# A three-pass feature-interaction kernel: second weights loaded one slot later, first weights in other buffers, one contraction row moved, chunk loops written out

## The reference

```python
# r_x: (2048, 39, 16); W0: (1, 39*39, 128); W1: (1, 39*128, 128)
x0 = x
xk = x
outs = []
for W in (W0, W1):
    Hk = xk.shape[1]                       # 39, then 128
    Wr = W.reshape(m, Hk, Hn)              # Hn = 128
    xk = jnp.einsum('bid,bjd,ijh->bhd', x0, xk, Wr)
    outs.append(xk)
result = jnp.concatenate(outs, axis=1)
return jnp.sum(result, axis=-1)            # (2048, 256)
```

## Time and profile before

| | us |
|---|---|
| median of 3 runs | 658.65 (657.7 to 661.69) |
| the profiled execution, its own time | 659.25 |
| its span (the trace) | 657.1 |
| busy in the span: PE / POOL / ACT / DVE | 577.2 / 482.4 / 475.5 / 469.9 |
| moved by DMA | 163.91 MB, mean 249 GB/s |

### The profile page before, as it was taken

One profiled execution on the slowest core, in us unless ns is written; L12 is line 12 of the kernel. 1 busy time (PEld: TensorE's weight loads), 2 busy tenths in 40 slices (PEclk: granted clock), 3 DMA queues, 4 the chain that ended last, 5 costly groups with the idle time before them and its releaser, 6 DMA issues.

```text
span 657.1 us, 12616 instructions
## 1 busy us (share of the span) xinstructions
PE 577.2 (88%) x3176; PEld 500.0 (76%) x3176; DVE 469.9 (72%) x806; ACT 475.5 (72%) x983; POOL 482.4 (73%) x407
## 2 busy tenths in 40 slices
PE   2475566677899999999997999999999999999988
PEld 1254445566788888888886888888888888888878
DVE  4564555455588888888886788888888888888730
ACT  4364645555688888888886888888888888888730
POOL 6765656555788888888885888888888889888700
PEclk9597787778899999999998999999999999999989
DMA  8865566666988899989996898989989898988110
GB/s 285 308 178 175 158 194 181 197 193 209 286 293 278 287 303 296 285 287 298 302 289 214 281 292 291 271 275 321 300 281 297 300 304 286 305 294 284 47 37 17
DMA packets 66357, 163.91 MB, mean 249 GB/s; under 512 B 10096, under 2 KB 18544, under 8 KB 66288
## 3 DMA queue, kind: packets, MB, share of 16 engines
q1 hardware_dynamic: 66288, 163.09, 77.7%
HBM read 139.98 MB, written 2.10 MB: 216 GB/s over the span
## 4 chain that ended last, share of the span: by engine, by line
PE 71%; DMA 13%; ACT 7%; DVE 3%; SPq 3%; issue 3%; POOL 1%; ACTq 0%; DVEq 0%
PE acc L361 13%; DMA xdr<-xd_dram 11%; PE acc L363 11%; PE acc L362 11%; PE fin L401 5%; PE fin L402 5%; PE fin L403 5%; PE pg L387 5%; PE pg L388 5%; PE pg L389 5%; PE turn L373 3%; ACT fh L454 3%; PE acc L356 2%; SPq L245 1%; DMA xr<-xb_dram 1%
## 5 line engine op out<-in xcount | busy, mean ns | idle before, releaser
L691 POOL TENSOR_TENSOR fl<-fs,fh 128x512 fp32r<-128x512 f32 x192 | 248.6, 1297 | 54.0 <-ACT fh L454 51.2
L361 PE MATMUL acc<-fh,w0h 128*128 128x512 f32 x384 | 170.5, 444 | 67.2 <-ACT x L475 49.6
L591 DVE TENSOR_TENSOR fl<-fp,fh 128x512 fp32r<-128x512 f32 x192 | 131.9, 687 | 84.7 <-ACT fh L454 80.9
L686 POOL TENSOR_TENSOR fs<-xr,xs 128x512 f32<-128x512 f32 x128 | 163.0, 1295 | 6.2 <-DMA xr<-xb_dram 6.2
L363 PE MATMUL acc<-fl,w0h 128*128 128x512 f32 x384 | 158.0, 411 | 0.0
L587 DVE TENSOR_TENSOR fp<-xl,xr 128x512 f32<-128x512 f32 x192 | 133.4, 696 | 34.3 <-ACT xl L461 24.0
L362 PE MATMUL acc<-fh,w0l 128*128 128x512 f32 x384 | 157.6, 410 | 0.0
L605 DVE TENSOR_TENSOR gl<-pg,gh 128x320 fp32r<-128x320 f32 x256 | 119.2, 486 | 38.7 <-ACT gh L494 36.2
L454 ACT ACTIVATE fh<-fp 128x512 fp32r<-128x512 f32 x192 | 114.1, 594 | 43.2 <-PE acc L363 38.4
L361 PEld LDWEIGHTS acc<-fh,w0h 128*128 128x128 f32 x384 | 76.0, 198 | 90.6 <-ACT x L475 53.2
L454 ACT ACTIVATE fh<-fs 128x512 fp32r<-128x512 f32 x192 | 121.0, 630 | 9.0 <-PE acc L363 7.6
(11 more groups left out here) (38 smaller groups left out, 748.5 us busy)
## 6 DMA issues: line engine op xcount, KB each, us to landing
xr<-xb_dram SPq DMA_DIRECT2D x192, 512.0 KB, 5.7
xbd<-xdhl SPq DMA_DIRECT2D x256, 80.0 KB, 3.8
xs<-xa_dram SPq DMA_DIRECT2D x64, 256.0 KB, 3.5
xdr<-xd_dram SPq DMA_DIRECT2D x64, 160.0 KB, 5.7
xp<-xpairs_dram SPq DMA_DIRECT2D x32, 256.0 KB, 3.9
outs<-w_dram SPq DMA_DIRECT2D x9, 256.0 KB, 2.7
out_dram<-outs SPq DMA_DIRECT2D x8, 256.0 KB, 5.0
xr<-w0a_dram SPq DMA_DIRECT2D x2, 256.0 KB, 5.2
```

The source lines that it names most:

```text
L361: nc.tensor.matmul(acc[:, :], w0h[:, t, :], fh[:, t, :], start=t == 0, stop=False)
L591: nc.vector.tensor_tensor(fl[:, t, :], f_at(t), fh[:, t, :], ALU.subtract).then_inc(low_dve, 1)
L686: nc.gpsimd.tensor_tensor(f_at(t), xr[:, gi % 2, t, :], xs[:, gi % 2, :], ALU.mult)\
L691: nc.gpsimd.tensor_tensor(fl[:, t, :], f_at(t), fh[:, t, :], ALU.subtract).then_inc(low_pool, 1)
```

## The change

1. `w1_load(g+1)` at the end of SP's slot g (from slot 0 on) becomes `w1_load(g)` (from slot 1 on). `w1_load(0)`, ahead of the slots, now stands behind a wait for `w0_ready` 3.
2. The first weights' raw pieces lie in other buffers: w0a in the tile of POOL's product 4 and in `outs`, w0b in `outs` and `x1`. SP's and POOL's order at the start is changed with it; the first squares and `low(0, 5)` are done ahead of slot 0.
3. Of each slot's rows of the contraction the first (EARLY = 1) is done behind quarters 0 and 1, ahead of `main` of tile 0; in the slots gi = 1 all five stay where they were.
4. The loops over chunks are written out on all engines.

```diff
--- before.py
+++ after.py
@@ -46,13 +46,15 @@
 W0_PART = 4
 W0_FROM = {0: 1, W0_PART: 2, FULL: 3}
 NW = 4
+EARLY = 1
 PIECES = -(-M // NW)
 
 
-def rows_of(s):
-
-
-    return range(IB * (s - 1), min(IB * s, M))
+def rows_of(s, late):
+
+
+    cut = IB * (s - 1) + (EARLY if s > 1 else 0)
+    return range(cut, min(IB * s, M)) if late else range(IB * (s - 1), cut)
 
 
 def piece(p):
@@ -141,9 +143,9 @@
         turn = ps("turn", [P, GC])
         xl = ps("xl", [P, GC])
         fp = ps("fp", [P, 2, GC])
-        w0a_raw = [xr[:, 1, NT - 2 + k, :].rearrange("p (t h) -> p t h", h=H) for k in range(2)]
-        w0b_raw = [outs[:, :, :].rearrange("p a b -> p (a b)").rearrange("p (t h) -> p t h", h=H),
-                   x1[:, :].rearrange("p (t h) -> p t h", h=H)]
+        outs_as_w = outs[:, :, :].rearrange("p a b -> p (a b)").rearrange("p (t h) -> p t h", h=H)
+        w0a_raw = [fs[:, SBUF_F[4], :].rearrange("p (t h) -> p t h", h=H), outs_as_w]
+        w0b_raw = [outs_as_w, x1[:, :].rearrange("p (t h) -> p t h", h=H)]
 
         ident_in = sem("ident_in")
         w0_sum = sem("w0_sum")
@@ -251,10 +253,11 @@
             def load_xd(g):
                 sp.dma_start(xdr[:, :, :, :], xd[g]).then_inc(xd_in, 16)
 
-            def w0_load(k):
-                ts = slice(W0_PART * k, W0_PART * k + W0_PART)
-                sp.dma_start(w0a_raw[k], w0a[:, ts, :]).then_inc(w0a_in[k], 16)
-                sp.dma_start(w0b_raw[k], w0b[:, ts, :]).then_inc(w0b_in[k], 16)
+            def w0a_load(k):
+                sp.dma_start(w0a_raw[k], w0a[:, W0_PART * k:W0_PART * k + W0_PART, :]).then_inc(w0a_in[k], 16)
+
+            def w0b_load(k):
+                sp.dma_start(w0b_raw[k], w0b[:, W0_PART * k:W0_PART * k + W0_PART, :]).then_inc(w0b_in[k], 16)
 
             def w1_load(p):
                 if p:
@@ -302,25 +305,27 @@
                         sp.wait_ge(xd_low, g + 2)
                     if more2:
                         load_xd(g + 2)
-                    if first or second and g + 1 < PIECES:
-                        w1_load(g + 1)
+                    if (first or second) and 0 < g < PIECES:
+                        w1_load(g)
                     if gi == 2 and not (first or second):
                         send(j - 2)
 
-            w0_load(0)
+            w0a_load(0)
+            w0b_load(0)
             load_x(0, 0)
             load_right(0, 0, 0)
             load_right(0, 0, 1)
-            w0_load(1)
+            w0b_load(1)
             load_right(0, 0, 2)
             load_pair(0)
-            load_xd(0)
             load_x(0, 1)
             load_right(0, 1, 0)
+            sp.wait_ge(w0_ready, 1)
+            w0a_load(1)
+            load_right(0, 1, 1)
+            load_right(0, 1, 2)
+            load_xd(0)
             sp.dma_start(idn[:, :], ident).then_inc(ident_in, 16)
-            load_right(0, 1, 1)
-            sp.wait_ge(w0_ready, 3)
-            load_right(0, 1, 2)
             wait_product(sp, 0, 0)
             wait_product(sp, 0, 4)
             load_x(0, 2)
@@ -331,11 +336,11 @@
             load_right(0, 2, 2)
             sp.wait_ge(xd_low, 1)
             load_xd(1)
-            sp.wait_ge(w0_sum, 1)
+            sp.wait_ge(w0_ready, 3)
             w1_load(0)
             chunk(0, True, False, False)
             chunk(1, False, True, False)
-            with sp.Fori(2, NCH - 1) as j:
+            for j in range(2, NCH - 1):
                 chunk(j, False, False, False)
             chunk(NCH - 1, False, False, True)
             send(NCH - 2)
@@ -389,6 +394,8 @@
                 nc.tensor.matmul(o, x1tl[:, q, :], xh, start=False, stop=True).then_inc(g_done, 1)
 
             def final(c, odd, rows, fresh):
+                if not rows:
+                    return
                 if rows[0] == 0:
                     pe.wait_ge(g_low, CB * NQ * (c + 1))
                     if not fresh:
@@ -404,6 +411,12 @@
                     if i == M - 1:
                         last.then_inc(fin_done, 1)
 
+            def last_rows(j, gi, first, second, odd, late):
+                if gi and not first:
+                    final(j - 1, not odd, rows_of(gi, late), second)
+                if not gi and not (first or second):
+                    final(j - 2, odd, rows_of(CB, late), False)
+
             def chunk(j, first, second, last, odd):
                 for gi in range(CB):
                     g = CB * j + gi
@@ -411,6 +424,7 @@
                     if not (first and gi < 2):
                         for q in (0, 1):
                             g_tile(j, gi - 2, q, first and gi == 2)
+                    last_rows(j, gi, first, second, odd, False)
                     main(j, gi, 0, fresh)
                     main(j, gi, 1, fresh)
                     if not (first and gi < 2):
@@ -422,22 +436,17 @@
                     main(j, gi, 3, fresh)
                     main(j, gi, 4, fresh)
                     main(j, gi, 5, fresh)
-                    if gi and not first:
-                        final(j - 1, not odd, rows_of(gi), second)
-                    if not gi and not (first or second):
-                        final(j - 2, odd, rows_of(CB), False)
+                    last_rows(j, gi, first, second, odd, True)
                     main(j, gi, FULL, fresh)
 
             chunk(0, True, False, False, False)
             chunk(1, False, True, False, True)
-            with pe.Fori(1, NCH // 2 - 1) as pair:
-                chunk(2 * pair, False, False, False, False)
-                chunk(2 * pair + 1, False, False, False, True)
-            chunk(NCH - 2, False, False, False, False)
+            for j in range(2, NCH - 1):
+                chunk(j, False, False, False, j % 2 == 1)
             chunk(NCH - 1, False, False, True, True)
             for q in (0, 1):
                 g_tile(NCH - 1, CB - 2, q, False)
-            final(NCH - 2, False, rows_of(CB), False)
+            final(NCH - 2, False, range(IB * (CB - 1), M), False)
             for q in (2, 3):
                 g_tile(NCH - 1, CB - 2, q, False)
             fill_turn(NG - 1, False)
@@ -518,8 +527,8 @@
                         g_high_part(j, gi - 2, 1, was_odd, None)
                     if more:
                         high(g + 1, 0, False)
-                    if gi % 2 == 0:
-                        squares(CP * j + gi // 2, first and gi == 0)
+                    if gi % 2 == 0 and prev:
+                        squares(CP * j + gi // 2, False)
                     if prev2:
                         g_high_part(j, gi - 2, 2, was_odd, None)
                     if more:
@@ -550,19 +559,18 @@
             high(0, 2, True)
             act.wait_ge(w0_sum, 2)
             nc.scalar.activation(w0h[:, W0_PART:NT, :], w0a_raw[1][:, 0:NT - W0_PART, :], COPY).then_inc(w0_high, 1)
+            high(0, 4, True)
+            high(0, 3, True)
+            high(0, 5, True)
+            squares(0, True)
             nc.scalar.activation(x1th[:, 0:2, :], w0a_raw[1][:, NT - W0_PART:W0_PART, :], COPY).then_inc(w0_high, 1)
             nc.scalar.activation(w0q[:, :, :], w0b_raw[1][:, NT - W0_PART:W0_PART, :], COPY).then_inc(w0_high, 1)
-            high(0, 4, True)
-            high(0, 3, True)
             xd_split(0, 0, True)
-            high(0, 5, True)
             left_out(0, 1, False)
             chunk(0, True, False, False, False)
             chunk(1, False, True, False, True)
-            with act.Fori(1, NCH // 2 - 1) as pair:
-                chunk(2 * pair, False, False, False, False)
-                chunk(2 * pair + 1, False, False, False, True)
-            chunk(NCH - 2, False, False, False, False)
+            for j in range(2, NCH - 1):
+                chunk(j, False, False, False, j % 2 == 1)
             chunk(NCH - 1, False, False, True, True)
             x1_out(NG - 1, False)
             g_high_part(NCH - 1, CB - 2, 0, True, None)
@@ -656,6 +664,7 @@
             nc.vector.tensor_tensor(w0l[:, W0_PART:NT, :], two, w0h[:, W0_PART:NT, :], ALU.subtract)\
               .then_inc(w0_ready, 1)
             low(0, 3)
+            squares_low(0)
             dve.wait_ge(w0_high, 4)
             last_lo = w0b_raw[1][:, NT - W0_PART:W0_PART, :]
             nc.vector.tensor_tensor(last_lo, last_lo, w0q[:, :, :], ALU.subtract).then_inc(w0_sum, 1)
@@ -663,10 +672,8 @@
             nc.vector.tensor_tensor(w0q[:, :, :], last_lo, x1th[:, 0:2, :], ALU.add).then_inc(w0_ready, 1)
             chunk(0, True, False, False)
             chunk(1, False, False, True)
-            with dve.Fori(1, NCH // 2 - 1) as pair:
-                chunk(2 * pair, False, False, False)
-                chunk(2 * pair + 1, False, False, True)
-            chunk(NCH - 2, False, False, False)
+            for j in range(2, NCH - 1):
+                chunk(j, False, False, j % 2 == 1)
             chunk(NCH - 1, False, True, True)
             for u in range(NQ):
                 g_low_part(NCH - 1, CB - 2, u, True)
@@ -713,7 +720,8 @@
```

(13 more changed lines are left out.)

## The result

The changed kernel takes 596.01 us in the median (591.47 to 604.08, 4 runs) against 658.17: ratio 0.903, interval 0.896 to 0.910. On a second chip it took 594.26 (591.59 to 596.73, 6 runs) against 659.19: 0.901, interval 0.897 to 0.906. One of the four executions, 604.08, counts as slow and is in the median but not in the ratio. The forecast was 594. The profiled execution has a span of 589.7 us, 67.4 less than before.

A forecast was written before the change was run, and what follows sets the result against it. The prediction took SP's wait for POOL's low part to bound the first ten steps, and PE after that. Span 657.1 - 48.6 - 4 - 10.2 - 2 = 592.3, forecast as a 594 us median, range 582 to 613.

The forecast's parts named there:

- Second weights one slot on: Ten slow steps, third to thirteenth xdr split: 9.2 us each instead of 14.06, saving 48.6 us (36 to 56).
- The longest of the four: Ten steps: transfers, 8.9 to 9.2 us a step, exceed POOL's 8.35, ACT's 7.7 and PE's 8.43.
- just in time: Rival: xd behind 1.1 MB of loads and a w1 piece makes ten steps 11.5 us each; 617 us, chance 0.07.
- Nothing flies while SP stands: Ten slow steps: no loads in flight while SP waits at w1_load for POOL's low part, 81.6 us in nine waits.
- The signs: Trace marks of being right: w1l wait 10 to 20 us, w1h pieces 8.7 to 9.8 us apart, clock 1.0 from third step.
- Start: First weights in other buffers and start reordered: -4 us (0 to -7).
- the quiet on the DMA engines can be won: Start: the 3 to 4 us in which the DMA engines are quiet can be saved.
- Loops and row: Loops written out: -10.2 us (-5 to -11); one contraction row behind the first quarters: -2 us.
- counter-term: Row: main's first third ends 0.36 us later for ACT's x1 copy, slack 0.21; could cost 23 x 0.17 = 3.9 us.
- the rival had it at half: Rival: PE clock stays at 1.2 GHz in the ten steps, 130 us instead of 92; 632 us, chance 0.03.
- the slower case: Rival: written-out code pays the 3.63 us stop at further instruction blocks; 685 us with 25 stops, chance 0.03.
- the ring: Ten slow steps: SP's issues, xd's flight, ACT and POOL in a 14.9 us loop; opening it saves 48.6 us.

The follow-up runs named there:

- The last experiment: Changed kernel with w0a_load(1) ahead of the pairs, x and first right half of group 1, and xd and its first split earlier: 597.53 us against 594.26.

## Why the prediction was right

- **Second weights one slot on.** Forecast 48.6 (36 to 56), measured 50.5 in the ten steps, 50.3 alone. The rate used, 300 to 310 GB/s, is the measured one: 301. "The longest of the four" is not shown: with less work on POOL or fewer bytes the steps came out no shorter than the runs differ. What the chain shows in late steps is the flight of the piece (5.9, 7.2 us) or of `xd`: the forecast's rival "just in time", in single steps. "Nothing flies while SP stands" is too strong: in the round of the earlier trace rows the burst was in flight until 93.64 us, and only the last 2.7 us of SP's wait had idle DMA engines (share 0.00). The 7.7 us a step from a higher rate is not what came, though 2 us stretches of the start moved up to 418 GB/s.
- **The signs.** "10 to 20 us of waiting for w1l" was wrong: it is 2.4, in four of nine rounds. SP reaches that wait behind its other waits and the issue of `xd`, and in the other five rounds POOL's low part was done by then. The pieces of `w1h` lie 7.8 to 9.7 us apart (8.7 to 9.8 forecast). The clock was 0.82 in the first and the sixth of the ten steps and 1.00 in the others, where 1.0 from the third on was forecast.
- **Start.** Forecast -4 (0 to -7), measured -1.5 at the third split (35.30 to 33.81), 1.2 to 2.7 over all traces. One step that failed is "comes perhaps 1 us later": DVE's sum came at 14.53 instead of 11.99, and the third part of the weights was ready at 20.5 instead of 17.7. The other is that the quiet on the DMA engines can be won. The second split did come 4.0 earlier, but the loads of slot 0, which wait for POOL's product 4 of group 1, went out at 22.97 (22.68 before) and the third `xd` at 27.93 (28.18 before). The quiet moved from 16 to 18 us (share 0.00) to 22 to 24 us (0.44). The last experiment repaired the sum and gained nothing.
- **Loops and row.** Forecast 10.2 and 2, measured 15.4 together after the thirteenth split. 1.1 of it is only the boundary: the next transposes follow that split after 6.29 instead of 7.43 us. Another 1.6 lies behind the last transposes, a stretch of 23.4 to 26.6 us over all traces, and of 24.2 and 26.4 in the two of the changed kernel. The turn was right in size (5.3 forecast; 13.85 became 8.4, 5.4), but not all of it is the stop of 3.63 that the prediction names: the clock behind the stop is the rest. During the stop not all engines stood: POOL was busy 3.1 us of it. Mis-attributed was the step: it went from 8.59 to 8.40 in the loops, about as the two terms together say, but either part alone takes it to 8.43. The forecast's mechanism for the row (0.31 against 0.23) was read in written-out code, where the row is worth 0.02 to 0.03 a step; in a loop that product takes 0.48. Its counter-term, ACT's late x1 copy (there 0.36 - 0.21 is 0.15, not 0.17), did not appear with one row.
- **Clock and code fetch.** The clock was 0.96 in the ten steps, where the rival had it at half. No 3.6 us stop is left on PE, so the slower case is out.

The mechanism of the main term was right. That the total met the 594 so closely is in part luck: the ring gave 1.9 us more than forecast, the start 2.5 less, loops, row, boundary and end 3.2 more, and the two medians, 596.01 and 594.26, differ by 1.8 themselves.

The sum of the four parts alone is 50.3 + 8.0 + 1.6 + 5.1 = 65.0 us; whole, 62.2 and 64.9 on two chips. In the traces the overlap of row and loops is 31 x 0.13 = 4 us (each alone takes 0.16 off a step, both 0.19); the medians are too coarse for it.

## What to carry to other kernels

When a DMA queue stands idle for microseconds in every step, look for the wait at the end of its slot: a wait for the result of the next slot makes a ring of issue, flight and compute, and moving one load by a slot opens it. Two cures for one gap do not add, so cost a pair of edits against the same row once. If a loop is to go for its turn's sake, it has to go on every engine that the step hangs on: PE alone or ACT alone in its loop kept nearly the whole cost. A stop of a few microseconds on PE is also paid in clock behind it.

## What the hardware showed that was not expected

- A load of 64 KB took 4.8 us to land and one of 256 KB 5.4, both behind other loads; 256 KB took 2.7 with nothing ahead.
- A looped PE starts later behind a wait: 8.60 against 8.44 us a step, by a first product of 0.48 instead of 0.31.
- The loop's turn costs PE the stop of 3.1 to 3.6 us and then 1.6 to 2.8 us more at the lower clock (granted 0.50 with PE looped).
- In two of fourteen traces DVE stood 7.47 us, both times at the low part of the squares, in written-out code, and the step became 18.4 and 18.5 us. The record of that operation is 8.86 us long, of which the chain counts 1.42 as work and 7.47 as "issue". One of them, DVE in order of time:

```profile
94.01 8.86 DVE L603 TENSOR_TENSOR sq<-xp,sq 64x512 fp32r<-64x512 f32 x1
```

  In the other twelve traces the operation's mean is 0.7 to 0.9 us. The cause stays open. Both were in the first chunks, which were written out before the change too.
